# A selective-scan kernel: even drives made by VectorE in PSUM, and expert rows scattered by GpSimd as they are made

## The reference

```python
x = x + attn_a(layernorm(x))      # attention on cos/sin of scaled Q and K
x = x + ffn(layernorm(x))         # mixture of 8 low-rank experts, top 2, for the first 2048 tokens
x = x + attn_b(layernorm(x))      # selective scan
x = x + ffn(layernorm(x))         # the same experts again

# ffn, for every (token, choice) pair, sorted by expert e:
h  = gelu(xr @ w1A[e].T @ w1B[e], approximate=False)
ye = h @ w2A[e].T @ w2B[e]
y[token] += weight * ye

# attn_b: x -> rmsnorm -> in_proj -> (u, z); u = silu(causal conv of 4 taps, 512 channels)
dt = softplus(dt_r @ dt_proj_w + b);  A = -exp(A_log)        # 16 states n per channel d
h[d, n] = exp(dt[d] * A[d, n]) * h[d, n] + dt[d] * u[d] * B[n]     # for every token
y[d]    = sum_n h[d, n] * C[n] + u[d] * D[d]
out     = (y * silu(z)) @ out_proj_w
```

## Time and profile before

| what | value |
|---|---|
| time, 3 runs | 2989.83, 2992.26, 2993.07 us; median 2992.26 us |
| profiled execution | 2989.16 us, span 2987.4 us |
| TensorE clock granted, mean | 0.961 |
| PE busy | 2668.5 us (89%) |
| DVE busy | 2348.1 us (79%) |
| ACT busy | 1848.3 us (62%) |
| POOL busy | 1826.3 us (61%) |
| transfers | 186.07 MB, mean 62 GB/s |
| attention | about 0 to 511 us |
| route and expert_ffn f1 | about 511 to 724 us |
| mamba before its first scan | 724 to 815 us |
| mamba, scans | 815 to 2718 us |
| rest of mamba, start of f2 | 2718 to 2775 us |
| f2 tile loop | 2775 to 2936 us |
| f2 gathering, adds, stores | 2936 to 2987 us |

### The profile page before, as it was taken

How to read it: one execution, slowest core, us unless ns; L and a number is a source line. 1 busy time by engine, 2 the same in 40 slices (tenths; PEclk the granted TensorE clock), 3 DMA queues, 4 the chain that set the end, 5 groups by cost and what they waited for, 6 DMA issues and landing times. The chain is left out here.

```text
span 2987.4 us, 48154 instructions
## 1 busy us (share of the span) xinstructions
PE 2668.5 (89%) x17342; PEld 2127.1 (71%) x17342; DVE 2348.1 (79%) x2434; ACT 1848.3 (62%) x2524; POOL 1826.3 (61%) x1211
## 2 busy tenths in 40 slices
PE   5999996596699999999999999999999999985892
PEld 4878785464277878878778788777787887874561
DVE  6878874574389889899888898998988988894563
ACT  3565653254567777777677776776777767761451
POOL 1221211454477877878778787787787877784454
PEclk8999998798799999999999999999999999998896
DMA  1211212424402112022020120210202202103333
GB/s 49 64 49 56 63 36 56 112 75 116 159 1 78 47 39 86 9 79 73 14 86 23 64 86 1 85 64 23 86 8 79 86 1 78 45 27 89 90 103 102
DMA packets 137133, 186.07 MB, mean 62 GB/s; under 512 B 27800, under 2 KB 112664, under 8 KB 136920
## 3 DMA queue, kind: packets, MB, share of 16 engines
q1 hardware_dynamic: 129432, 162.69, 17.8%
q0 software_dynamic: 7488, 20.46, 2.7%
HBM read 141.13 MB, written 41.98 MB: 61 GB/s over the span
## 5 line engine op out<-in xcount | busy, mean ns | idle before, releaser
L1353 POOL TENSOR_TENSOR m_state<-m_state,m_c_all 128x1024 f32<-128x1024 f32 x512 | 1205.1, 2368 | 357.3 <-DVE m_state L1468 356.3
L1468 DVE TENSOR_TENSOR_SCAN m_state<-m_decay,m_ps_d 128x1024 f32<-128x1024 f32 x512 | 1162.1, 2278 | 145.0 <-issue 89.0
L1533 ACT ACTIVATE m_decay<-m_dt,m_aneg 128x511 f32<-128x511 f32 x1024 | 657.7, 710 | 30.1 <-DVE m_state L1468 26.6
L1768 PEld LDWEIGHTS m_ps_d<-m_bdiag,m_duT 128*128 128x128 f32 x4096 | 488.4, 192 | 105.9 <-issue 73.4
L1781 PE MATMUL m_ps_y<-m_ident,m_state 128*128 128x128 f32 x4096 | 533.1, 273 | 3.0 <-POOL m_state L1353 2.5
L1768 PE MATMUL m_ps_d<-m_bdiag,m_duT 128*128 128x128 f32 x4096 | 504.5, 276 | 29.4 <-DVE m_state L1468 23.6
L1781 PEld LDWEIGHTS m_ps_y<-m_ident,m_state 128*128 128x128 f32 x4096 | 463.6, 141 | 8.7 <-POOL m_state L1353 7.5
L1445 DVE TENSOR_TENSOR m_duB<-m_duT,m_ps_i 128x1024 f32<-128x1024 f32 x256 | 306.1, 1196 | 8.8 <-ACT m_duT L1561 8.8
L1766 PEld LDWEIGHTS m_ps_d<-m_ident,m_duB 128*128 128x128 f32 x2048 | 235.5, 141 | 76.9 <-issue 70.9
L1679 PE MATMUL m_ps_f<-m_hT,m_win 128*128 128x512 f32 x512 | 249.8, 612 | 36.0 <-ACT m_u L1574 17.9
L1766 PE MATMUL m_ps_d<-m_ident,m_duB 128*128 128x128 f32 x2048 | 265.8, 273 | 7.1 <-DVE m_state L1468 7.0
(11 more groups left out here) (201 smaller groups left out, 4407.0 us busy)
## 6 DMA issues: line engine op xcount, KB each, us to landing
m_c_all<-m_c_rows SPq DMA_DIRECT2D x128, 512.0 KB, 5.5
out<-m_xw SPq DMA_DIRECT2D x32, 512.0 KB, 2.9
f_y_rows<-f_y_sb SPq DMA_DIRECT2D x46, 256.0 KB
a_xin<-x SPq DMA_DIRECT2D x16, 512.0 KB, 4.8
a_xres<-x SPq DMA_DIRECT2D x16, 512.0 KB, 5.6
x<-a_xout SPq DMA_DIRECT2D x16, 512.0 KB, 3.3
m_xin<-x SPq DMA_DIRECT2D x16, 512.0 KB
m_xw<-out SPq DMA_DIRECT2D x16, 512.0 KB, 5.6
```

Of the source, the lines that this page charges most:

```text
L1353: nc.gpsimd.tensor_tensor(s, s, c_all[:, n, :, :], ALU.mult).then_inc(weighed, 1)
L1468: nc.vector.tensor_tensor_scan(state[:, r, :, :].rearrange("p n t -> p (n t)"), decay[:, r, :, :].rearrange("p n t -> p (n t)"), ps_d[i % ...
L1533: ins = nc.scalar.activation(decay[:, r, j, 1:S], dt_sb[:, c, 1:S], ACT.Exp, scale=aneg[:, c, n:n + 1])
L1768: ins = nc.tensor.matmul(drive_t, duT[:, c, t, :], bdiag[:, n // 2, TT * j + t, :], start=True, stop=True)
```

## The change

Two parts.

**Mamba.** Even units get their drive from VectorE alone. `du` is put into PSUM once per channel block (`put_du`, on ScalarE), B is broadcast to all partitions by four more transfers per item (`b_all`), and `scale` multiplies the two straight into `ps_d[0]`, which only VectorE now writes and reads. The eight transposes of each even unit go from TensorE, and the extra copy of B into PSUM goes from VectorE. The four diagonals of an item move: two to GpSimd (one instruction each, after units 26 and 28), two to ScalarE (8 activations each, at steps 0 and 3). `dt` and `duT` are held for two blocks in place of four. Turns and steps from 16 to 24 shift by one (table below). The decay constants are turned by TensorE from one plain load instead of 16 small transfers.

**Experts.** The route now gives for each row of a tile the row of its pair (`pair_row`; unused rows go to a spare block of 128). GpSimd scatters each half tile from one of three `y_sb` to `y_rows` in pair order, each scatter waiting for the one before it to have landed. The copy of the first weights (`ranks_in`) comes before the gathers, that of the others (`downs_in`) behind them. In the second call and in `mamba` eight plain loads of 512 KB bring the rows back.

The expert block, its tensor of rows and SyncE:

```diff
-    y_rows = nc.dram_tensor(tag + "y_rows", [MT * TS, D], F32, kind="Internal").ap()
+    y_rows = nc.dram_tensor(tag + "y_rows", [P + TOK * TOPK, D], F32, kind="Internal").ap()
...
-            for j in range(MT):
...
-                sp.wait_ge(y_ready, j + 1)
-                sp.dma_start(y_rows[j * TS:(j + 1) * TS, :].rearrange("(h p) d -> p h d", p=P),
-                             y_sb[j % 2][:, :, :]).then_inc(y_stored[j % 2], 16)
...
+            sp.wait_ge(y_stored, 16 * NH)
+            for g in range(NT // YG):
+                for k in range(TOPK):
+                    sp.dma_start(y_back[:, k * NT + g * YG:k * NT + (g + 1) * YG, :],
+                                 y_rows[P + k * TOK + g * YG * P:P + k * TOK + (g + 1) * YG * P, :]
+                                 .rearrange("(t p) d -> p t d", p=P)).then_inc(y_got[g], 16)
```

The expert block, GpSimd:

```diff
+            def scatter(j, h):
+                n = HS * j + h
+                if h == 0:
+                    pool.wait_ge(y_ready, j + 1)
+                if n:
+                    pool.wait_ge(y_stored, 16 * n)
+                nc.gpsimd.indirect_dma_start(y_rows, bass.IndirectOffsetOnAxis(pair_row[:, n:n + 1], 0),
+                                             y_sb[j % YR][:, h, :], None).then_inc(y_stored, 16)
...
             for j in range(MT):
                 if j + 2 < MT:
                     power(j + 2)
+                if j + 1 < MT:
+                    ranks_in(j + 1)
+                if j >= 2:
+                    scatter(j - 2, 1)
                 if j + XR < MT:
                     fetch(j + XR)
                 if j + 1 < MT:
-                    stage(j + 1)
...
-            for t in range(NT):
-                for k in range(TOPK):
-                    c = k * NT + t
-                    nc.gpsimd.indirect_dma_start(y_back[:, c, :], None, y_rows,
-                                                 bass.IndirectOffsetOnAxis(places[:, c:c + 1], 0))\
-                        .then_inc(y_got[t // YG], 16)
+                    downs_in(j + 1)
+                if j:
+                    scatter(j - 1, 0)
+            scatter(MT - 2, 1)
+            for h in range(HS):
+                scatter(MT - 1, h)
+            pool.wait_ge(y_stored, 16 * NH)
```

mamba, SyncE:

```diff
-            for r in range(Q):
-                for k in range(CT):
-                    sp.dma_start(aneg[CH * r:CH * r + CH, k, :].rearrange("c (q g) -> c q g", q=Q),
-                                 a_log[:, Q * k + r, :].rearrange("(c q) g -> c q g", q=Q)).then_inc(a_loaded, 16)
+            for g in range(NTK // YG):
+                for k in range(TOPK):
+                    sp.dma_start(ex_y[k][:, YG * g:YG * (g + 1), :],
+                                 ROUTE["y_rows"][P + k * TOK + YG * g * P:P + k * TOK + YG * (g + 1) * P, :]
+                                 .rearrange("(t p) d -> p t d", p=P)).then_inc(ex_got[g], 16)
...
+            def b_pair(m):
+
+                sp.dma_start(b_all[:, m, :, :], bc_rows[0, 4 * m:4 * m + 2, :].partition_broadcast(P))\
+                    .then_inc(b_loaded[m], 16)
```

mamba, VectorE (`scale`):

```diff
-                nc.vector.tensor_tensor(duB[:, r, :, :, :], duT[:, c, :, :].unsqueeze(1).to_broadcast([P, 2, TT, P]),
-                                        ps_bt[h][:, 2 * n:2 * n + 2, :].unsqueeze(3).to_broadcast([P, 2, TT, P]),
-                                        ALU.mult).then_inc(scaled, 1)
+                if i >= 2 or st.has(o - 1):
+                    dve.wait_ge(scanned, UN * b + i - 1)
+                nc.vector.tensor_tensor(ps_d[0][:, :, :], ps_u[:, :].unsqueeze(1).to_broadcast([P, 2, S]),
+                                        b_all[:, n // 2, :, :], ALU.mult).then_inc(scaled, 1)
```

mamba, ScalarE (`put_du`, and the body of `diagonal`):

```diff
+            def put_du(st, o, c):
+
+                b = st.item(o)
+                act.wait_ge(du_ready, CT * b + c + 1)
+                if c or st.has(o - 1):
+                    act.wait_ge(scaled, UN // 2 * b + NP // 2 * c)
+                nc.scalar.activation(ps_u[:, :], du_sb[:, c % 2, :], ACT.Copy).then_inc(du_put, 1)
...
+                for j in range(2):
+                    for t in range(TT):
+                        ins = nc.scalar.activation(bdiag[:, n // 2, TT * j + t, :], id_sb[:, :], ACT.Copy,
+                                                   scale=bt[h][:, 2 * n + j, t:t + 1])
```

mamba, TensorE (`drive` and its call):

```diff
-                        drive_t = ps_d[i % 2][:, j, t * P:(t + 1) * P]
-                        if n % 2 == 0:
-                            ins = nc.tensor.transpose(drive_t, duB[:, i // 2 % SR, j, t, :], id_sb[:, :])
-                        else:
-                            ins = nc.tensor.matmul(drive_t, duT[:, c, t, :], bdiag[:, n // 2, TT * j + t, :],
-                                                   start=True, stop=True)
+                        ins = nc.tensor.matmul(ps_d[1][:, j, t * P:(t + 1) * P], duT[:, c % DR, t, :],
+                                               bdiag[:, n // 2, TT * j + t, :], start=True, stop=True)
...
-                    if i < UN - 1 and st.has(0):
+                    if i % 2 == 0 and st.has(0):
                         drive(st, 0, i + 1)
```

The table of turns:

```diff
-        16: [("O", 0, -1)],
-        18: [("X", 0, 1)],
-        19: [("Y", 1, 0), ("DU", 3, 0)],
-        20: [("B", 0, 1)],
-        21: [("DT", 0, 1)],
-        22: [("O", 1, -1)],
+        17: [("O", 0, -1)],
+        19: [("X", 0, 1)],
+        20: [("Y", 1, 0), ("DU", 3, 0)],
+        21: [("B", 0, 1)],
+        22: [("DT", 0, 1)],
+        23: [("O", 1, -1)],
```

More of the change, by code:

```diff
@@ L458, in expert_ffn @@
     XR = 4
+    YR = 3
     YG = 4
@@ L512, in expert_ffn @@
         y_full, y_ready = sem("y_full"), sem("y_ready")
-        y_stored = [sem(f"y_stored{r}") for r in range(2)]
+        y_stored = sem("y_stored")
         y_got = [sem(f"y_got{g}") for g in range(NT // YG)]
@@ L563, in expert_ffn @@
                 list_f = rt("list_f", [P, NH])
+                token_f = rt("token_f", [P, NH])
+                later = rt("later", [P, NH])
                 passed = rt("passed", [P, MT, E])
@@ L711, in expert_ffn @@
         c_sb = [sb(f"c_sb{r}", [P, TS]) for r in range(2)]
-        y_sb = [sb(f"y_sb{r}", [P, HS, D]) for r in range(2)]
+        y_sb = [sb(f"y_sb{r}", [P, HS, D]) for r in range(YR)]
         block = ctx.enter_context(nc.Block())
@@ L1479, in emit @@
                         y_read(st, 0, (i - 9) // 8)
-                    if i == 0 and st.has(0):
-                        diagonal(st, 0, NP - 1)
                     if i in (9, 17) and st.has(0):
@@ L1485, in emit @@
                         gate(st, -1, 3)
-                    if i in (17, 23) and st.has(-1):
-                        b, v = st.item(-1), (i - 17) // 6
+                    if i in (18, 24) and st.has(-1):
+                        b, v = st.item(-1), (i - 18) // 6
                         dve.wait_ge(res_back, 16 * (b + 1))
@@ L1626, in emit @@
                         nc.scalar.activation(xd[0:RX, :], f_bank("X", 0)[0:RX, :], ACT.Copy).then_inc(xd_ready, 1)
-                    if i == 21 and st.has(1):
+                    if i == 22 and st.has(1):
                         b = st.item(1)
@@ L1661, in _ @@
         def _(pe):
+            pe.wait_ge(a_loaded, 16 * 3)
+            for r in range(Q):
+                for q in range(Q):
+                    ins = nc.tensor.matmul(ps_a.rearrange("p (k q g) -> p k q g", q=Q, g=G)[CH * r:CH * r + CH, :, q, :],
+                                           id_sb[:, bass.ds(q, CH, step=Q)], a_nat[:, bass.ds(r, CT, step=Q), :],
+                                           start=True, stop=True, skip_group_check=True)
+            ins.then_inc(placed, 1)
+            for k in range(CT):
+                ins = nc.tensor.matmul(ps_u[RX:RX + 1, k * P:(k + 1) * P], b_nat[:, k:k + 1], id_sb[:, :],
+                                       start=True, stop=True)
+            ins.then_inc(placed, 1)
             pe.wait_ge(w_loaded, 16 * 4)
@@ L1722, in turn @@
                     f = take(st, kind, k)
+                    if not st.has(0):
+                        pe.wait_ge(bias_set, 1)
                     pe.wait_ge(xd_ready, b + 1)
@@ L1787, in emit @@
                 for i in range(UN):
-                    if i < UN - 1 and st.has(0):
+                    if i % 2 == 0 and st.has(0):
                         drive(st, 0, i + 1)
-                    if i == UN - 1 and st.has(1):
-                        drive(st, 1, 0)
                     if i >= 2 and st.has(0):
```

271 lines of the change are left out of this document (135 added, 136 removed).

## The result

| | before | changed | ratio (95% interval) |
|---|---|---|---|
| first comparison, 13 and 13 runs | 2991.01 us | 2981.38 us | 0.9967 (0.9959 to 0.9975) |
| once more (e8_after), 13 and 4 runs | 2991.36 us | 2980.77 us | 0.9958 (0.9941 to 0.9974) |

The account below looks back on a forecast made before the run. TensorE was taken as the scans' bound, VectorE close behind, GpSimd pacing the expert loop. Scans -131, first expert call +12, second -10, before the first scan -7: -136 from 2989.2 gives 2853 us, range 2795 to 2940.

Parts of the forecast that it names:

- The work in an item: In a scan item: TensorE 102 us, VectorE 103.8, GpSimd 98, ScalarE 95; VectorE's product 1.24 us.
- the one from the two sums to the item: Scan item: larger engine of each pair of units adds to 112.7 us, larger queue sum is 103.3; same share gives 109.
- Six tenths: Scan item: the old item, 119.9 us, lay six tenths between 115.8 and 122.5; the same share was applied again.
- the fifth: Scan item: held by some other order, transposes only filled gaps, 119.9 us stays, total 2987 us; chance 0.03.
- The clock: In the scans, a sign of being wrong: clock below 1.00, where TensorE is less busy; no size given.
- Rival 2: ScalarE or GpSimd becomes the bound at the scan item's edge: 115 us an item, total 2913; chance 0.17.
- The expert loop: In each expert call: a tile takes 7.3 us against 6.95, scatter landing 1.8 us; +6 us a call.
- Rivals 3 and 4: Expert tiles: scatters land later than gathers, at 3.6 us, total 2941 (chance 0.10), or 5.4 us, 3092 (chance 0.06).
- The end of f1: First expert call: four scatters in a row, last down 8 us after the last y_sb, against 2.4; +6 us.
- The end of f2: Second expert call: plain loads replace the 32 gathers, end at about 2971.5 us against 2987; -16 us.
- Before the first scan: Start of mamba: eight loads replace gathers and small loads, done by about 765 us; -7 us, within -18 and +5.

Follow-up runs that it names:

- e8_after: The changed kernel measured once more, against the kernel before in the same job: 2980.77 us, ratio 0.9958.
- e13_order_flat: e5_order with the scan's items written out one after the other in place of the hardware loop; 2812.40 us, ratio to the kernel before 0.9458.
- e5_order: The changed kernel, every instruction kept, only the steps moved at which queues issue them, 52 numbers; 2854.49 us, ratio to the kernel before 0.9537.
- the five tried: The changed kernel with first silu of V at step 7, `xw` 26, `xin` 30, Y turn 18, GpSimd's norm 15; ratio to the kernel before 0.9832.
- e10_silu7: The changed kernel with ScalarE's first silu of V at step 7, not 6; ratio to the kernel before 1.0011.

## Why the prediction was wrong

- **The work in an item** was right, engine by engine: product 1.23 us (1.24), VectorE 103 (103.8), ScalarE 93.4 (95), GpSimd 96.2 (98), TensorE 105 in e13_order_flat at full clock (102).
- **The failed step is the one from the two sums to the item**: "The larger of each pair adds to 112.7, the larger sum is 103.3 ... The same share gives 109 us now." The item was 120.0 us and not 111: 9.3 us went to the order of the queues and 2.7 to the turns of the loop, and the step has a term for neither. Six tenths was fitted to one kernel, where TensorE was busy 98% of the time; with a bound engine almost any rule gives its sum. It also took the larger of two engines in a pair as a ceiling. Without the turns the item is 117.3, above that ceiling, and with another order the same instructions take 108.05, below my 109. ScalarE's queue was left out of the lists, and the scans wait for its decays in the one order (26.6 us) and not in the other (0.2). That the old order fails because it was laid for a TensorE that is never free is my reading; which of the 52 moves matter beyond the five tried is open.
- **The rival that came true is the fifth**, at 0.03: "the item is held by some other order ... and 119.9 stays". I let 98% of TensorE speak against it. That row shows what bounded the old kernel; it says nothing of the order once TensorE is relieved. No run lays the kernel before in another order; with TensorE busy 116.8 us in an item of 119.9 it had some 3 us to gain at most.
- **The clock** stood in the text as a sign of being wrong, but with no price. In e5_order an item with a turn and low clock costs 5.2 us more than its neighbours, and the turn itself had no term at all.
- **Rival 2**, ScalarE at the edge: the wait was 2.3 us of a possible 2.5, and moving `xin` and one Y turn gave 1.5 us. It is there, and makes a sixth of the miss.
- **The expert loop**: landing right, tile 7.7 for 7.3, because a scatter behind a wait is recorded up to 1.57 us. Rivals 3 and 4 are out: the last scatters' waits of 1.7 and 2.2 us are the landing. The rule of the Trainium skill that spoke for them (DMA: Bandwidth & Descriptors; 2.0 us plus bytes) lies near these and not near 3.6. (The last gather of the earlier trace rows takes 2.76 us from issue to use, where the prediction writes 2.6.)
- **The end of f1**: +14.7 for +6. The last scatter was down 9.3 us after the last y_sb (forecast 8); the drain of 7.58 us was not in the sum. **The end of f2**: -19.3 for -16; the drain is there too, beside the loads.
- **Before the first scan**: -16.7 for -7, right in sign, inside its bounds, and only in jobs where the gathers are slow. In the others the changed kernel should be slower than before; e10_silu7, which is the changed kernel but for one move without effect, stands at 1.0011 there. So the sign of the whole result was luck.

## What to carry to other kernels

When a change relieves the engine that is the bound, its gain is not the difference of the sums: the order of the other queues was made around the old bound, and has to be laid anew before the sum is worth anything. Follow each in-order queue with its waits, all engines at once, and price a hardware loop's turn and the clock after a pause as terms of their own. And split an edit before judging it: the copy ahead of the gathers was worth 10 us a call, and was hidden by the scatters that came with it.
